# A decoder layer of 32 token groups: new engine orders and PSUM banks, head copies by DMA, GpSimd's small operations on ScalarE

## The chip, the cores and the metric

One core of a Trainium2 chip runs the whole kernel. The metric is the device time of one execution in microseconds (us).

## The reference, cut to what matters

x is 128 x 64 x 128 in float32 (128 sequences of 64 tokens, 128 channels), and so is the context.

```python
x = x + self_attention(layernorm(x))          # 16 heads of 8, RoPE, causal, softmax, output projection
x = x + cross(layernorm(x), ctx)              # Q K^T / dk, no softmax, times V; Wo; residual; layernorm with gain
x = x + ffn(layernorm(x))                     # 8 experts, top 1: h = relu(xhat_e W1_e^T + b1); y = x + h W2_e^T + b2
# in RoPE a head's 8 channels are two halves of 4: (x1 cos - x2 sin, x1 sin + x2 cos)
# in ffn: assign = argmax(x @ centroids.T), alpha = sigmoid(x @ centroids.T), out = alpha*y + (1 - alpha)*x
```

## The kernel before, in words

The 8192 tokens are 32 groups (`NG`) of 256 tokens (`J` = 2 tiles of 128 rows). The first two thirds of the program treat the groups; the rest is the feed-forward part, 71 blocks of 128 rows each, gathered by expert from a DRAM buffer `expert_rows` and scattered to the output.

Every engine has a function `one(g)`, a list of lines `stage(g, back, op)`, which `rounds` repeats: in round i an engine carries out each op for group i - back, in the order of the list. So a group passes through about nine rounds, and the order of the list is the order of the engine's program. Engines meet only by semaphores: `wait(engine, steps, group, "name")` waits until the named step of that group is done. The tables `BANK` (which of the 8 PSUM banks an op uses), `BEFORE` and `DRAIN` (whose reads must be over before a bank is written) belong to one order of the lists.

What happens to a group, with the names that the profile shows:

- SyncE's queue (SPq) loads x (`load_x`, tile `xin`), x again for the residual (`load_again`, `xr`) and the context (`load_ctx`, `cin`). Its function `late_loads(i)` runs after `one` in round i: three constants at i = 0, ten loads of biases and cross weights at i = 1 (semaphore `d_bias`), the mask `mk` and four others at i = 4, and one expert weight of 256 KB in each of the rounds 10 to 25.
- VectorE (DVE) takes the statistics (`stats_x`), ScalarE (ACT) and GpSimd (POOL) normalise, TensorE (PE) turns x (`x_turned`) and makes Q and K (`queries_keys`).
- DVE multiplies with cos and sin (`rotate`) and swaps partner partitions by a shuffle (`partners`, tile `t_`), POOL adds the two (`rotated`, tile `qk`).
- ACT makes four copies of `qk` (`by_head`, tile `ex`), each with the rows of three heads in four multiplied by 0 (`own4`), which spreads the heads for TensorE's tiles.
- PE builds the scores twice: once for the row maxima (`max_scores`, in front L691 and L701), which DVE reduces (`row_max`, L1432), and once with the maxima subtracted (`scores`, L733, L739, L747), which ACT exponentiates (`exp`, tile `prob`). `weighted` (L764) multiplies with V (tile `vau`, written by `values`, L678); DVE turns it back, POOL divides, `projected` (L791, L795) makes the output.
- Cross attention (`ctx_turned`, `cross_keys_values`, `values_keys`, `x1_turned`, `cross_queries`, `attended`, `cross_output`) and routing (`affinities`, `largest`, `ranks`, slot numbers, `scatter_rows`) follow in later rounds. Small tiles of 128 x 2 (variances, their roots) are worked on by POOL: `std_x`, `std_x1`, `std_y`, `std_x2`.

Two waits stand early in the program. PE's `constants()` runs inside `queries_keys` of group 1 and needs the ten loads of `d_bias`. DVE's `setup(4)` reads the mask.

Of the kernel before, what the change touches and what calls it, by code (L numbers as in the profile page):

```python
# [144 lines left out]
def decoder_kernel(nc, x, ctx, mask, wself, wcross, bcol, brow, cent, w1t, lngb, b1c, w2t, b2r,  # L145
# [17 lines left out]
    with es:  # L163
# [11 lines left out]
        WQ, WQR, WK, WKR, WV, WO = (ws[:, i, :] for i in range(6))  # L175
# [21 lines left out]
        own4, own4s = cf[:, o:o + 4], cf[:, o + 4:o + 8]  # L197
# [71 lines left out]
        sc = two("sc", [P, J, 3])  # L269
        tm = two("tm", [P, J, 3, E])  # L270
# [74 lines left out]
        ac_f = stage_steps("act_front", "xT | V0 V1 | x0 x1 x2 x3 | hi")  # L345
        ac_a = stage_steps("act_exp", "e0 | e1")
        ac_t = stage_steps("act_cross", "cT | kv | n | xT | Q2 | A | s0 s1")
        ac_r = stage_steps("act_route", "id | ea al1 | neg")
# [6 lines left out]
        dv_r = stage_steps("dve_route", "w0 w1 | b0 b1 a0 a1 | ab | af | g | i0 i1 | f | o | al | rk | tot | pr | sl | si")  # L355
        po_l = stage_steps("pool_norm_x", "eps pow")
        po_f = stage_steps("pool_front", "qk | lo")
        po_a = stage_steps("pool_attention", "n0 n1")
        po_t = stage_steps("pool_cross", "eps neg pow mr | x1b | eps2 std pow2 | zg")
        po_r = stage_steps("pool_route", "eps eps2 pow | R mr | z")  # L360
        d_x = [sem(f"dma_x{i}") for i in range(2)]
        d_xr = [sem(f"dma_x_again{i}") for i in range(2)]
        d_c = [sem(f"dma_ctx{i}") for i in range(2)]
        d_s = [sem(f"dma_scatter{i}") for i in range(2)]
# [18 lines left out]
        s_clear = sem("setup_cleared")  # L383
# [39 lines left out]
        def rounds(one, count, early=None):  # L423
# [11 lines left out]
            "x_turned": bank[6],  # L435
            "x1_turned": bank[4],
            "cross_keys_values": bank[7],
            "ranks": bank[6],
            "cross_queries": bank[4],
            "ctx_turned": bank[5],  # L440
            "queries_keys": bank[7],
            "attended": bank[6],
            "max_rows": bank[4],
            "projected": bank[5],
# [4 lines left out]
            "cross_output": bank[4],  # L449
            "values_keys0": bank[5],  # L450
            "values_keys1": bank[6],
            "weighted": bank[7],
            "values": bank[4],
# [9 lines left out]
        N_CONST, N_BIAS, N_LATE, N_WEIGHTS = 3, 10, 4, 2 * E  # L463
# [3 lines left out]
        SETUP = bank[3]  # L467


        EARLY_AT = (NG - 4, NG - 1, NG, NG + 1, NG + 2, NG + 3)  # L470
# [8 lines left out]
        def _(sp):  # L479
# [96 lines left out]
        def _(pe):  # L576
# [11 lines left out]
                "x_turned": [(dv_t, "mt", -3), (ac_t, "A", -5), (dv_r, "tot", -7), (ac_f, "xT", -1)],  # L588
                "x1_turned": [(ac_f, "V1", 3), (dv_t, "y1", -1), (ac_s, "x", 1), (ac_t, "Q2", -1),
                    (ac_t, "xT", -1)],  # L590
                "cross_keys_values": [(dv_a, "ot", -1), (dv_f, "k2", 1), (ac_t, "kv", -1)],
                "ranks": [(ac_f, "xT", 6), (dv_t, "mt", 3), (ac_t, "A", 1), (dv_r, "tot", -1)],
                "cross_queries": [(ac_t, "xT", 0), (ac_f, "V1", 3), (dv_t, "y1", -1), (ac_s, "x", 1),
                    (ac_t, "Q2", -1)],
                "ctx_turned": [(dv_t, "mt", -3), (dv_t, "x1", -4), (ac_t, "cT", -1)],
                "queries_keys": [(ac_t, "kv", -2), (dv_a, "ot", -3), (dv_f, "k2", -1)],
                "attended": [(dv_r, "tot", -2), (ac_f, "xT", 4), (dv_t, "mt", 1), (ac_t, "A", -1)],
                "max_rows": [(ac_t, "Q2", -2), (ac_t, "xT", -2), (ac_f, "V1", 1), (dv_t, "y1", -3),
                    (ac_s, "x", -1)],
                "projected": [(ac_t, "cT", 3), (dv_t, "mt", 0), (dv_t, "x1", -1)],  # L600
                "scores0": [(dv_s, "m0", 0), (ac_a, "e0", -1)],
                "scores1": [(dv_s, "m0", 0), (ac_a, "e0", -1)],
# [1567 lines left out]
```

## Time and profile before

| | |
|---|---|
| runs | 604.33, 600.85, 602.0 us; median 602.0 |
| profiled execution | 606.41 us, of which the span is 604.2 |
| TensorE, granted clock | 0.981 of full speed over the span |
| busy shares | PE 90%, DVE 80%, ACT 77%, POOL 72% |
| first and last group's first `weighted` on PE | at 31.98 and 423.94 us |

Times inside the span count from its start. Between the first and the last of these `weighted` lie 31 rounds; what follows is the feed-forward part. The engines' busy shares are means over both.

### The profile page before, as it was taken

To read this page: it belongs to the slowest core of one execution; us is meant where nothing else is said; L and a number is where in the kernel's file an instruction comes from. 1 tells how busy PE (TensorE), PEld (TensorE's weight loads), DVE (VectorE), ACT (ScalarE), POOL (GpSimd) and SP (SyncE) were. 2 spreads that over 40 slices of the span, in tenths; PEclk is the share of its full clock that TensorE was granted. 3 is DMA by queue.
4 is the path that set the end of the run, shared out by engine and by line. 5 is a ranking of instruction groups with operands and counts; after the bars stand their busy time and mean duration, and the time that the engine had idled before them with its cause. 6 is when DMAs were issued, how large, how long until landed. Compare 5 with 4: busy or idle time off the path is not lost.

```text
span 604.2 us, 26574 instructions
## 1 busy us (share of the span) xinstructions
PE 543.7 (90%) x8719; PEld 430.0 (71%) x8719; DVE 485.4 (80%) x1762; ACT 463.6 (77%) x1304; POOL 434.1 (72%) x852
## 2 busy tenths in 40 slices
PE   4789999999999999999999999978887988999995
PEld 2467767766766666676676666756786977999894
DVE  3787999888998989998899998987676666777673
ACT  2777777877888878888778787775776775899893
POOL 3334788888988989888998888877665566354553
PEclk9799999999999999999999999999899999999999
DMA  6421111322112312122111121102112122322210
GB/s 174 56 77 30 29 38 39 96 68 58 54 56 78 88 56 56 55 84 81 55 38 40 51 62 38 30 20 71 28 47 60 52 65 70 83 72 67 60 54 14
DMA packets 55189, 35.46 MB, mean 59 GB/s; under 512 B 14976, under 2 KB 50433, under 8 KB 55056
## 3 DMA queue, kind: packets, MB, share of 16 engines
q1 hardware_dynamic: 50160, 24.44, 15.5%
q0 software_dynamic: 4320, 8.66, 4.3%
q8 instruction: 74, 1.21, 0.8%
q10 hardware_dynamic: 576, 0.66, 0.4%
q14 instruction: 59, 0.48, 0.3%
HBM read 24.46 MB, written 9.74 MB: 57 GB/s over the span
## 4 chain that ended last, share of the span: by engine, by line
PE 84%; issue 6%; ACT 3%; DVE 3%; SPq 1%; another core or an unknown queue 1%; DVEq 1%; DMA 0%; POOLq 0%; POOL 0%; ACTq 0%
PE side L963 9%; PE side L764 8%; PE quad L701 6%; PE side L668 5%; PE quad L733 5%; PE side L948 5%; PE quad L948 5%; PE side L825 5%; PE side L678 3%; PE side L861 3%; PE side L879 3%; PE side L833 2%; PE side L795 2%; PE quad L747 2%; PE side L846 2%
## 5 line engine op out<-in xcount | busy, mean ns | idle before, releaser
L2046 POOL DMA_INDIRECT out<-yo,rb x71 | 69.9, 984 | 74.9 <-DVE yo L1784 45.6
L963 PE MATMUL side<-w,hT 128*128 x568 | 79.5, 284 | 8.7 <-DVE hT L1574 6.8
L1073 ACT ACTIVATE ex<-qk,cf 128x512 f32<-128x512 f32 x128 | 85.4, 718 | 0.0
L1432 DVE TENSOR_REDUCE mx<-quad 128x16 f32<-128x1024 f32 x64 | 75.3, 1218 | 10.9 <-PE quad L701 10.8
L963 PEld LDWEIGHTS side<-w,hT 128*128 128x128 f32 x568 | 71.5, 197 | 11.6 <-issue 11.0
L2013 POOL DMA_INDIRECT expert_rows<-pay,sli x64 | 68.6, 1072 | 12.8 <-issue 12.8
L1092 ACT ACTIVATE prob<-quad 128x1024 f32<-128x1024 f32 x64 | 62.1, 1022 | 18.6 <-PE quad L747 18.6
L764 PE MATMUL side<-prob,vau 128*32 128x64 f32 x2048 | 50.9, 223 | 14.5 <-issue 12.6
L764 PEld LDWEIGHTS side<-prob,vau 128*32 128x32 f32 x2048 | 36.7, 109 | 24.9 <-issue 17.0
L1564 DVE TENSOR_SCALAR xh<-rb 128x128 f32<-128x128 f32 x71 | 25.1, 354 | 27.8 <-issue 24.4
L1189 ACT COPY w1b<-w 128x512 f32 x71 | 43.7, 617 | 0.0
L948 PE MATMUL quad<-xhT,w1b 128*128 128x128 f32 x288 | 40.6, 287 | 2.0 <-issue 2.0
L1167 ACT ACTIVATE xhT<-quad,gb 128x128 f32<-128x128 f32 x71 | 33.2, 468 | 11.0 <-PE quad L931 7.4
L948 PEld LDWEIGHTS quad<-xhT,w1b 128*128 128x128 f32 x288 | 37.4, 202 | 2.3 <-issue 2.2
L1046 ACT COPY xT<-side 128x256 f32<-128x256 f32 x32 | 11.9, 372 | 35.2 <-PE side L659 35.2
L948 PE MATMUL side<-xhT,w1b 128*128 128x128 f32 x280 | 37.8, 278 | 1.0 <-ACT xhT L1167 1.0
L701 PE MATMUL quad<-ex,qk 32*64 32x256 f32 x1024 | 38.4, 396 | 0.1
L668 PE MATMUL side<-xT,ws 128*128 128x256 f32 x128 | 36.1, 405 | 1.8 <-ACT xT L1046 0.7
L948 PEld LDWEIGHTS side<-xhT,w1b 128*128 128x128 f32 x280 | 35.1, 196 | 1.7 <-ACT xhT L1167 1.2
L733 PE MATMUL quad<-ex,qk 32*64 32x256 f32 x1024 | 35.8, 387 | 0.2 <-DVE vau L1330 0.2
L1985 POOL TENSOR_TENSOR pay<-ve,half 128x4 f32<-128x4 f32 x32 | 33.4, 1042 | 2.7
L1197 ACT ACTIVATE bs<-rb 128x128 f32<-128x128 f32 x71 | 35.1, 495 | 0.0
(276 smaller groups left out, 1610.2 us busy)
## 6 DMA issues: line engine op xcount, KB each, us to landing
rb<-expert_rows SPq DMA_DIRECT2D x71, 68.0 KB
xin<-in_x SPq DMA_DIRECT2D x32, 128.0 KB
cin<-in_ctx SPq DMA_DIRECT2D x32, 128.0 KB
xr<-in_x SPq DMA_DIRECT2D x32, 128.0 KB, 2.3
w<-in_w1t SPq DMA_DIRECT2D x8, 256.0 KB
w<-in_w2t SPq DMA_DIRECT2D x8, 256.0 KB
out<-yo,rb POOLq DMA_INDIRECT x71
expert_rows<-pay,sli POOLq DMA_INDIRECT x64
```

The source lines that it names most:

```text
L668: last = mm(BANK["queries_keys"][:, i * TG:(i + 1) * TG], w, xT[g.par][:, :], start=True, stop=True)
L701: last = mm(quad[64 * b:64 * b + 64, r_, 256 * j:256 * j + 256], qk[g.par][strip, 0, own], ex[g.par][strip, :, 1, own], start=False, stop= ...
L733: mm(quad[64 * b:64 * b + 64, r_, 256 * j:256 * j + 256], qk[g.par][strip, 1, own], ex[g.par][strip, :, 0, own], start=j == 0, stop=False, ...
L764: last = mm(to[32 * i:32 * i + 32, j, :, r_, :], vau[g.par][:, j, 4 * r_ + i, :], prob[g.par][:, r_, (4 * j + i) * SQ:(4 * j + i + 1) * SQ ...
L948: last = mm(HT[u][c // 2][:, (c % 2) * P:(c % 2 + 1) * P], w1b[u][:, c * P:(c + 1) * P], xhT[u][:, :], start=True, stop=True)
L963: last = mm(YB[u][:, 0:D], hT[u][:, c, :], w2[:, bass.ds(e, 1), c, :], start=c == 0, stop=c == FC - 1)
L1073: act(ex[g.par][:, i, :, :].rearrange("p a t -> p (a t)"), qk[g.par][:, :, :].rearrange("p a t -> p (a t)"), ACT.Copy, scale=own4[:, i:i + ...
L1092: act(prob[g.par][:, 2 * h_:2 * h_ + 2, :], quad[:, 2 * h_:2 * h_ + 2, :], ACT.Exp).then_inc(*ac_a.done(f"e{h_}"))
L1189: cp(w1b[u][:, :], w1[:, bass.ds(e, 1), :].rearrange("p e f -> p (e f)")).then_inc(*ffn["act_w1"].done("act_w1"))
L1432: v.tensor_reduce(mx[g.par][:, 2 * h_:2 * h_ + 2, :], quad[:, 2 * h_:2 * h_ + 2, :].rearrange("p r (h k) -> p r h k", k=SQ), AX.X, ALU.max ...
L2013: v.indirect_dma_start(out=rows, out_offset=bass.IndirectOffsetOnAxis(ap=sli[g.par][:, j:j + 1], axis=0), in_=pay[g.par][:, j, :], in_offs ...
L2046: v.indirect_dma_start(out=o_rows, out_offset=bass.IndirectOffsetOnAxis(ap=number, axis=0), in_=yo[b.c % 4][:, :], in_offset=None, bounds_ ...
```

## The change: what it does

**Heads.** The columns of the Q and K weights are permuted on the chip when the means are subtracted, so that in a strip of 32 partitions head i holds the partitions i, i+4, i+8, ... The shuffle swaps partitions 16 apart instead of 4 apart, and the tables for cos, sin and the biases are loaded in that order, by eight DMAs on ACT's queue. ACT's four scaled copies per group are gone: `ex` is set to zero once, and four DMAs per group on SP's queue copy every fourth partition of `qk` into it (`by_head`).

**GpSimd's small operations.** Six operations of 128 x 2 per group (the additions of epsilon and one negation) go from POOL to ACT. The product of the affinity scores with their scales goes from one DVE operation to four small ones on ACT, `place` on DVE becomes a matmul in `ranks`.

**Orders.** All lists of stages are new, with the banks and their tables. ACT's stages stand one round later, DVE's one round earlier; the loads of SP move too.

```diff
+            def by_head(g):
+                first(sp, g, s_clear, 2)
+                wait(sp, pe_s, g.n - 2, "s3")
+                wait(sp, pe_a, g.n - 2, "s3")
+                wait(sp, po_f, g.n, "qk")
+                for i in range(4):
+                    sp.dma_start(ex[g.par][i:P:4, i, :, :], qk[g.par][i:P:4, :, :]).then_inc(d_by[g.par], 16)
             def one(g):
-                stage(g, 2, load_ctx)
-                stage(g, 3, load_again)
+                stage(g, 4, load_again)
                 stage(g, 0, load_x)
-            rounds(one, NG + 3, early=late_loads)
+                stage(g, 1, by_head)
+                stage(g, 0, load_ctx)
+            rounds(one, NG + 4, early=late_loads)
...
-                wait(pe, ac_f, g.n, "x3")
+                wait_dma(pe, d_by, g, 4)
...
+                wait(pe, dv_r, g.n - 1, "tot")
+                mm(bank_[:, 0:(J + 1) * E].rearrange("p (a e) -> p a e", e=E), identf,
+                   cnt[:, :].unsqueeze(1).broadcast_to((P, J + 1, E)), start=True, stop=False)
...
-            def by_head(g, part_):
...
-                for i in part_:
-                    act(ex[g.par][:, i, :, :].rearrange("p a t -> p (a t)"),
-                        qk[g.par][:, :, :].rearrange("p a t -> p (a t)"), ACT.Copy, scale=own4[:, i:i + 1]
-                        ).then_inc(*ac_f.done(f"x{i}"))
...
+            def var_x(g):
+                wait(ac, po_l, g.n - 2, "pow")
+                wait(ac, dv_l, g.n, "a1")
+                act(ve["L"][g.par][:, :], mv["L"][g.par][:, :, 1], ACT.Copy, bias=EPS).then_inc(*ac_v.done("eL"))
...
-            ac.dma_start(cf[:, 0:i0], consts[:, 0:i0]).then_inc(d_rope, 16)
-            ac.dma_start(bc[:, :], bcol).then_inc(d_rope, 16)
+            for r_ in range(4):
+                own = slice(32 * r_, 32 * r_ + 32)
+                ac.dma_start(cf[own, 0:4 * SQ], consts[own, 0:4 * SQ].rearrange("(i m) c -> m i c", i=4)
+                             ).then_inc(d_rope, 16)
+                ac.dma_start(bc[own, 0:4], bcol[own, 0:4].rearrange("(i m) c -> m i c", i=4)).then_inc(d_rope, 16)
+            ac.dma_start(cf[:, 4 * SQ:i0], consts[:, 4 * SQ:i0]).then_inc(d_rope, 16)
+            ac.dma_start(bc[:, 4:6], bcol[:, 4:6]).then_inc(d_rope, 16)
...
-                                 [p ^ (HD // 2) for p in range(32)]).then_inc(*dv_f.done("sh"))
+                                 [p ^ 16 for p in range(32)]).then_inc(*dv_f.done("sh"))
...
-            def scaled_scores(g):
...
-                v.tensor_tensor(tm[g.par][:, :, :, :],
...
-                u = ve["L"][g.par]
                 wait(po, ac_l, g.n - 2, "n")
-                wait(po, dv_l, g.n, "a1")
-                v.tensor_scalar(u[:, :], mv["L"][g.par][:, :, 1], EPS, None, ALU.add).then_inc(*po_l.done("eps"))
```

**TensorE's order.** The first rows are a piece of one steady round of before, in program order (L846 is `values_keys`, L764 `weighted`, L678 `values`, L691 and L701 `max_scores`, L659 `x_turned`).

```order
L846 MATMUL side<-kv_0 64x64 x7
L764 MATMUL side<-prob,vau 32x2x32 [waits act_cross_kv,dve_front_q1,dve_attention_ot,act_front_V0,act_exp_e0]
L764 MATMUL side<-prob,vau 32x2x32 x15
L678 MATMUL side<-ws,xT 128x128 [waits act_cross_Q2,act_cross_xT,act_maxima_x,act_front_V0,dve_cross_y1,act_front_xT]
L764 MATMUL side<-prob,vau 32x2x32 [waits act_exp_e1]
L764 MATMUL side<-prob,vau 32x2x32 x15
L691 MATMUL quad<-late_k,row_q 128x8x32 x7
L701 MATMUL quad<-ex,qk 64x256 [waits act_front_x0]
L659 MATMUL side<-cf,xn 128x128 [waits dve_route_tot,act_cross_A,act_front_xT,dve_cross_mt,act_norm_x_n]
```

The next rows are a piece of a steady round of the changed kernel; its lines are some five higher (L866 `attended`, L851 `values_keys`, L877 to L884 `cross_output`, L769 `weighted`, L696 and L706 `max_scores`, L782 `ctx_turned`, L664 `x_turned`, L683 `values`).

```order
L866 MATMUL side<-q_0,mt_0 64x64 x7
L851 MATMUL side<-kv_0 64x64 x7
L877 MATMUL side<-bo,ones_b 128x304 [waits dve_cross_x1]
L880 MATMUL side<-gc,xT_0 128x16 x2
L884 MATMUL side<-wcx,av 128x136 [waits act_cross_A]
L769 MATMUL side<-prob,vau 32x2x32 [waits act_cross_A,act_front_V0,act_exp_e0]
L769 MATMUL side<-prob,vau 32x2x32 [waits act_exp_e1]
L696 MATMUL quad<-late_k,row_q 128x8x32 [waits act_exp_e1,act_exp_e0]
L706 MATMUL quad<-ex,qk 64x256 [waits dma_by_head1]
L782 MATMUL side<-cf,cin 128x128 [waits dve_cross_y1,dma_ctx1]
L664 MATMUL side<-cf,xn 128x128 [waits dve_cross_mt,act_norm_x_n]
L683 MATMUL side<-ws,xT 128x128 [waits dve_attention_ot,act_front_xT]
```

`values` has left the gap between the two halves of `weighted`, `attended` and `values_keys` stand together, and the wait of `max_scores` for ACT's copy x0 is a wait for the DMAs of `by_head`.

**SP's queue at the start.** These are its first loads in the kernel before.

```order
L516 DMA xin<-in_x 128x2x128
L487 DMA cf<-in_consts 128x279
L487 DMA nkf<-in_negk 128x64
L493 DMA br<-in_brow 128x768
L493 DMA wcx<-in_wcross 128x512
L493 DMA gc<-in_cent 128x8
L493 DMA ln_c<-in_brow 128x1 x3
L495 DMA wop<-in_wself 32x1x128 x4
```

And these, after the first two loads of x and the constants, are those of the changed kernel.

```order
L541 DMA ex<-qk 32x512 [waits pool_front_qk,setup_cleared_heads]
L541 DMA ex<-qk 32x512 x3
L530 DMA cin<-in_ctx 128x2x128
L493 DMA br<-in_brow 128x768
L493 DMA wcx<-in_wcross 128x512
L493 DMA gc<-in_cent 128x8
L493 DMA ln_c<-in_brow 128x1 x3
L495 DMA wop<-in_wself 32x1x128 x4
```

The ten loads of `d_bias` stand behind the copies of group 0, which wait for `rotated` of group 0.

**The mask.** This piece is SP's queue of the changed kernel in its round 4, up to the mask (the copies are those of group 3).

```order
L516 DMA xin<-in_x 128x2x128 [waits act_norm_x_n]
L541 DMA ex<-qk 32x512 [waits pool_front_qk,pe_attention_s0,pe_scores_for_max_s0]
L541 DMA ex<-qk 32x512 x3
L530 DMA cin<-in_ctx 128x2x128 [waits pe_cross_cT]
L500 DMA mk<-in_mask 128x64x16
L502 DMA gb<-in_lngb 128x16
```

And this is DVE's program of the changed kernel around its first use of the mask (the shuffle is that of group 3).

```order
L1514 TENSOR_TENSOR x_0<-side,xr 128x256 [waits pe_cross_out,dma_x_again0]
L1528 TENSOR_TENSOR mt_1<-side,headmask 128x256 [waits pe_cross_gram]
L1471 STREAM_SHUFFLE t__1<-t__1 128x512 [waits dve_front_q1,pool_front_qk]
L1741 TENSOR_REDUCE pen<-mk 128x64 [waits dma_mask]
L1743 TENSOR_SCALAR pen<-pen 128x64 [waits setup_mask]
L1387 CAST part<-br 128x256
L1491 STREAM_TRANSPOSE ot<-side 128x512 [waits pe_attention_p1]
```

In before the mask's load had only loads of x and context ahead of it. Now copies that wait for POOL, and a load that waits for PE's `ctx_turned` of group 2, stand ahead of it.

## Rows read from the trace of the kernel before

**Rows 1.** The page: the chain that ended last, share of the span by engine

```profile
PE 84%; issue 6%; ACT 3%; DVE 3%; SPq 1%; another core or an unknown queue 1%; DVEq 1%; DMA 0%; POOLq 0%; POOL 0%; ACTq 0%
```

**Rows 2.** PE's timeline (start, us, what): the first group's weighted, the last one's

```profile
31.98 0.65 PE L764 MATMUL side<-prob,vau 128*32 128x64 f32 x32 [0.75 <-ACT prob L1092]
...
423.94 1.11 PE L764 MATMUL side<-prob,vau 128*32 128x64 f32 x42
```

**Rows 3.** The chain in one round, 252.4 to 265.1: start, us, what

```profile
253.29 1.10 PE side L668 x4
...
259.37 0.59 PE side L764 x28
259.95 0.45 issue
260.40 0.33 PE side L764 x4
260.73 0.64 PE side L678 x4
...
263.34 0.37 PE side L659 x2
263.71 0.22 PE side L808 x2
```

**Rows 4.** Windows: the same round; busy PE, PEld, DVE, ACT, POOL; PEclk, DMA share

```profile
252.50:265.00 12.50, 11.89 (x237) 8.69 (x235) 11.24 (x42) 10.16 (x29) 11.24 (x25) 1.00 0.23 67
```

**Rows 5.** Waits of DVE and PE, 120 to 360, 19 rounds: us, times, longest

```profile
DVE ot L1442 <- PE side L764: 7.0, 17, 0.5
DVE mx L1432 <- PE quad L701: 6.3, 19, 0.9
DVE y L1492 <- PE side L879: 4.9, 19, 0.4
...
PE side L764 <- issue: 8.3, 19, 0.5
```

**Rows 6.** Groups by line: busy us, mean ns of one, idle before

```profile
L1073 ACT ACTIVATE ex<-qk,cf 128x512 f32<-128x512 f32 x128 | 85.4, 718 | 0.0
L1159 ACT ACTIVATE ea<-ea 128x2 f32<-128x2 f32 x32 | 6.5, 204 | 1.0
L1903 POOL TENSOR_SCALAR ve_L<-mv_L 128x2 f32<-128x2 f32 x32 | 7.6, 237 | 5.2 <-DVE mv_L L1298 5.2
L1517 DVE TENSOR_TENSOR tm<-y,sc 128x48 f32<-128x48 f32 x32 | 6.9, 216 | 0.0
```

**Rows 7.** SP's queue and DVE's use of xin in a round that loads weights

```profile
256.93 0.47 SPq L516 DMA_DIRECT2D xin<-in_x  x1
257.44 0.47 SPq L509 DMA_DIRECT2D w<-in_w1t  x1
...
261.11 0.49 DVE L1295 BATCH_NORM_STATS2 stat_L<-xin 128x6 f32<-128x128 f32 x2 [0.35 <-DMA xin<-in_x]
```

**Rows 8.** DMA issues: KB each, median us from issue to landing

```profile
xr<-in_x SPq DMA_DIRECT2D x32, 128.0 KB, 2.3
...
mk<-in_mask SPq DMA_DIRECT2D x1, 512.0 KB, 6.9
```

**Rows 9.** The start: SP's bias loads, first and last, and POOL's first qk

```profile
3.17 0.47 SPq L493 DMA_DIRECT2D br<-in_brow  x1
...
6.06 2.87 SPq L495 DMA_DIRECT2D wop<-in_wself  x4
...
16.26 1.27 POOL L1915 TENSOR_TENSOR qk<-t__0 128x512 f32<-128x512 f32 x1 [5.43 <-DVE t__0 L1422]
```

**Rows 10.** The start on PE (constants) and DVE (shuffle, mask)

```profile
19.68 0.77 PE L649 MATMUL quad<-ws,bvx 128*128 128x128 f32 x2 [2.75 <-ACT tri_b L1033]
...
30.85 0.73 DVE L1422 STREAM_SHUFFLE t__0<-t__0 128x512 f32<-128x512 f32 x1
...
32.38 1.21 DVE L1718 TENSOR_REDUCE pen<-mk 128x64 f32<-128x1024 int32 x1
```

More of the change, by code:

```diff
@@ L174, in decoder_kernel @@
         ws = sb("ws", [P, 6, D])
-        WQ, WQR, WK, WKR, WV, WO = (ws[:, i, :] for i in range(6))
+        WQP, WKP, WV, WO = (ws[:, i, :] for i in (1, 3, 4, 5))
         wcx = sb("wcx", [P, 4 * D + E])
@@ L363, in decoder_kernel @@
         d_c = [sem(f"dma_ctx{i}") for i in range(2)]
+        d_by = [sem(f"dma_by_head{i}") for i in range(2)]
         d_s = [sem(f"dma_scatter{i}") for i in range(2)]
@@ L434, in decoder_kernel @@
             "max_scores3": bank[3],
-            "x_turned": bank[6],
-            "x1_turned": bank[4],
-            "cross_keys_values": bank[7],
-            "ranks": bank[6],
[L439 to L444, printed above, removed]
+            "ctx_turned": bank[4],
+            "x_turned": bank[5],
+            "values": bank[7],
+            "x1_turned": bank[6],
+            "cross_keys_values": bank[4],
+            "ranks": bank[6],
+            "queries_keys": bank[5],
+            "cross_queries": bank[7],
+            "max_rows": bank[6],
             "scores0": bank[0],
@@ L448, in decoder_kernel @@
             "scores3": bank[3],
-            "cross_output": bank[4],
+            "projected": bank[4],
+            "attended": bank[7],
             "values_keys0": bank[5],
             "values_keys1": bank[6],
+            "cross_output": bank[4],
             "weighted": bank[7],
-            "values": bank[4],
         }
@@ L896, in one @@
                 stage(g, 4, max_scores)
+                stage(g, 4, ctx_turned)
                 stage(g, 2, x_turned)
+                stage(g, 3, values)
                 stage(g, 6, x1_turned)
@@ L1727, in _ @@
             v.memset(row_q[:, :, :, :], 0.0)
-            v.memset(row_kk[:, :, :, :], 0.0).then_inc(s_clear, 1)
-            rounds(one, NG + 4, early=setup)
+            v.memset(row_kk[:, :, :, :], 0.0)
+            v.memset(ex[0][:, :, :, :], 0.0).then_inc(s_clear, 1)
+            rounds(one, NG + 3, early=setup)
             def last_table(k):
@@ L1870, in _ @@
             rows_in(Block(2))
-            place(g28)
+            own_rank(g28)
             counted(g28)
@@ L1909, in rotated @@
             def rotated(g):
-                wait(po, ac_f, g.n - 2, "x3")
+                wait_dma(po, d_by, g.back(2), 4)
                 wait(po, pe_s, g.n - 2, "s3")
```

353 lines of the change are left out of this document (169 added, 184 removed).

## The prediction

> **What bounds the kernel now.** I read the chain first: TensorE (PE) holds 84% of it and "issue" 6% [rows 1], so the time is PE's program, and no other engine's wait runs through it for long. Next I took the timeline, to see how the span divides. The first group's `weighted` stands at 31.98 and the last one's at 423.94 [rows 2]: 31 rounds of 12.64 us, a start of 32 and a feed-forward tail of 180 us. The change leaves the tail's matmuls alone, so three numbers matter: the start, the length of a round, and whether the tail keeps its 180.
>
> For the round I took the chain over one of them. Its pieces add up to 12.55, nearly all PE, with one "issue" of 0.45 in the middle of `weighted`, behind which four matmuls take 0.33 [rows 3]. It comes back in every round [rows 5]. Nothing that the profile knows of is missing there, so I read it as instructions that come late. In the same 12.5 us DVE is busy for 11.24, ACT for 10.16, POOL for 11.24 [rows 4]. The waits say how near DVE is: over 19 rounds it stands still for 7.0 + 6.3 + 4.9 = 18.2, about 1.0 per round [rows 5], so its own work, gaps between instructions included, takes 11.5. A change that shortens PE's round has 1.0 us before it meets DVE.
>
> **The rounds, part by part.** *ACT.* Four copies of 718 ns go [rows 6], 2.9 us per round. Ten operations of 128 x 2 or x 8 come, at 204 ns like its own small ones [rows 6], 2.0. ACT goes from 10.2 to 9.3 and does not bind, either way. *POOL* loses six operations at about 237 ns [rows 6], 1.4 us, and goes from 11.24 to below 10. *DVE* loses two of at most 216 ns [rows 6]: 11.5 - 0.4 = 11.1. That is the floor that DVE sets.
>
> *PE.* The order has 12 changes of tile shape per round before and 9 after, counted along both lists. What one costs I read from two turnings of a tile that are alike: L659 behind a shape change 0.37, L808 behind its own kind 0.22 [rows 3], so 0.15. I priced every group anew by whether it now stands behind its own shape. `x_turned` saves 0.15; `values`, 0.64 between two halves of `weighted` and now behind `x_turned`, 0.19; the second half of `weighted`, `values_keys`, the turned maxima and `cross_queries` 0.11 to 0.16 each (0.56). `ctx_turned`, the output's bias and that of `cross_output` now follow a change and pay 0.15 + 0.11 + 0.06. Of the 1.10 of `queries_keys` (L668), 0.22 was a wait for the bank of the cross keys, which it leaves. The matmul added to `ranks` costs 0.18. The sum is -0.15 - 0.19 - 0.56 + 0.32 - 0.22 + 0.18 = -0.62, and the round becomes 11.93. This keeps the "issue" and its slow matmuls, 0.45 + 0.33 less the 0.1 that four matmuls cost elsewhere. If they vanish, PE needs 11.3 and DVE's 11.1 is next.
>
> The Trainium skill, in the page "TensorEngine Tiling (Array Packing)", section Key Properties, says that a change of the tiling mode, not merely of the tile, drains TensorE. The 0.15 in [rows 3] agrees. By the rule alone one would price only the three changes fewer, 0.45, and with the added matmul the round would become 12.28; this is the last rival below.
>
> *The queue.* The four copies are now DMAs on SP's queue, and there they stand ahead of the next load of x. This closes a loop of exactly one round: `rotated` of a group ends, four issues at 0.51 from start to start [rows 7] make 2.0, `load_ctx` 0.5, `load_again` 0.5, then x takes 2.3 from issue to landing, as the residual's load of the same size does [rows 8]. DVE's statistics wait for it, and in DVE's new list everything up to `partners` stands behind them: 4.2 by its operations. Then POOL's 1.3 for `rotated` [rows 9], and the loop is closed: 2.0 + 0.5 + 0.5 + 2.3 + 4.2 + 1.3 = 10.8. That is below 11.93 and costs nothing. In the 16 rounds that load an expert's weights one more issue of 0.5 stands in it, and landing is slower: in such a round x went out at 256.93 and DVE stood until 261.11, 4.2 us [rows 7]. The loop is then 11.3 with a landing of 2.3 and 13.2 with one of 4.2. I take 12.2, between the two, since the weights now go out 1.0 ahead of x instead of behind it. The mean round is (15 x 11.93 + 16 x 12.2) / 31 = 12.07, bounds 11.3 and 12.6. The rounds give back 31 x (12.64 - 12.07) = 17.7 us.
>
> **The start, part by part.** *Biases.* The ten loads went out from 3.17 to 8.9 [rows 9], long before PE's constants at 19.68, which waited for something else [rows 10]. Now they stand behind the copies of group 0, which wait for POOL's `qk`. That ended at 17.5 [rows 9]; ACT issues eight more DMAs ahead of its first work at 0.5 to 0.7 each (the last four bias loads, with the same kind of pattern, took 2.87 [rows 9]), so I put it at 21.5. Then 2.0 for the copies, 0.5 for the context, 5.8 for the ten loads and 2.3 for landing: 32.1. PE's constants stand in `queries_keys` of group 1, ahead of the first `max_scores`. All behind them is late by 32.1 - 19.7 = 12.4, so the first `weighted` comes at 44. Bounds: 8 if ACT's DMAs delay nothing, 17 if the biases land as slowly as the mask's 6.9 [rows 8].
>
> *The mask.* DVE read it at 32.38 without a wait [rows 10]. Now DVE wants it right behind the shuffle of group 3, and its load stands behind the copies of the same group, which wait for what POOL makes of that very shuffle: 1.3 + 2.0 + 0.5 + the landing of 6.9 [rows 8] = 10.7 of standstill on DVE, more if `ctx_turned` of group 2, for which the context's load waits, is late. Behind it in DVE's program are the turned outputs and the next row maxima, for which PE and ACT wait soon; about 1.7 are hidden by PE's rest of a round. I take 9, bounds 6 and 14.
>
> *Back.* The first eight rounds have fewer operations than a steady one, and a program that is late by its latencies catches up in them a little: -3, an estimate, bounds 0 and -6. The start costs 12.4 + 9 - 3 = 18.4, bounds 10 and 28.
>
> *The tail* holds the same matmuls; the leftover small operations change places only. Zero, within 2 us either way, covered by PE's own chain there.
>
> **The sum.** 606.4 (the profiled execution) + 18.4 - 17.7 = 607.1. The profiled execution lies 4.4 above the median of the runs, so against the median it is 602.0 + 0.7: about 602, no change that can be measured. A measurement of this kernel tells a change from none at about 0.5%, 3 us.
>
> **The rivals.**
> - *The rounds save more, or the start costs less (faster).* If the missing instructions were a matter of the old order, PE drops to 11.3; coupled to DVE's 11.1 the round is about 11.5, and 31 x 1.14 = 35 are saved: 602 - 35 + 18 = 585. If only the start is cheaper, at its bound of 10, 594. For it speaks that the stall comes once in each of 19 rounds, always in `weighted` [rows 5], and the new order has other neighbours there; against it, that the two halves of `weighted` and the 48 matmuls behind them now follow each other without a pause. Chance 0.24.
> - *SP's queue sets the round (slower).* The place is `load_x` behind the four copies, the price is what the loop has beyond PE's 11.93. From a mean round of 12.64 - 18.4/31 = 12.05 on the kernel is slower. With the landing of 4.2 in weight rounds (13.2) and 11.93 else, the mean is 12.6 and the time 602 - 1 + 18 = 619; half of that excess gives 610. For it: DVE already stood for x once in such a round [rows 7]. Against it: x's load was last in the queue before weights then. Chance 0.22.
> - *The shape's grouping gives only its three drains.* Round 12.28, so 31 x 0.36 = 11 saved, 602 - 11 + 18 = 609; 615 if the stall of 0.45 grows in the now longer dense stretch by 0.2. For it: the groups' first matmuls overlap with the drain of the group ahead, so savings of 0.1 to 0.2 may be read twice. Chance 0.14.
>
> **How the numbers follow.** The forecast (start 15 to 22, round 11.9 to 12.2) has 0.40 and runs from 594 to 609, with 602 its middle: 0.13 of it below 599, 0.15 within 3 us of the 602, 0.12 above. The first rival lies from 580 to 594 nearly whole. The second covers 606 to 620, the third 605 to 616. Faster: 0.24 + 0.13 = 0.37. Same: 0.15 + 0.04 from the low ends of the others and 0.03 from the high end of the first = 0.22. Slower: the rest, 0.41. The range takes in all of the forecast and leaves out a tenth at either end: 586 to 617.
>
> **What the profile of the changed kernel would show.** The first `weighted` near 44 instead of 31.98, and PE's constants near 32 waiting for the bias loads; DVE's reduction of the mask behind a wait of about 10 us for its DMA, and PE idle by it. Rounds of 11.9 to 12.2 from the first `weighted` to the last; DVE's waits for PE down to 0.8 per round; in weight rounds a wait of the statistics for x. In the chain L659 at 0.22, L678 at 0.45 and "issue" of 0.45 near `weighted`. I am wrong if the first `weighted` stands below 38 or above 50, if the rounds lie below 11.7 or above 12.3, or if DVE has the mask when it asks for it.

## The result

The changed kernel takes 671.0 us (median of 667.07 to 673.08) against 603.16 for the kernel before on the same chip: a ratio of 1.112, 95% interval 1.106 to 1.119. The forecast of 602 was wrong, and so was its range. Its profiled execution has a span of 670.6 us, 66.4 longer than before.

The page of the changed kernel shows first that no single engine holds the end any more: PE's share of the chain is 39% where it was 84% [rows 1], and SP's queue, DMA, DVE and POOL have a part in it.

```profile
PE 548.1 (82%) x8783; PEld 444.6 (66%) x8783; DVE 490.5 (73%) x1701; ACT 439.2 (65%) x1496; POOL 388.6 (58%) x659
...
PE 39%; DVE 17%; issue 14%; SPq 10%; DMA 8%; POOL 5%; ACT 3%; ACTq 2%; DVEq 2%; another core or an unknown queue 0%; POOLq 0%
```

Next the timelines of its start (start, duration, engine, line): SP's copies and bias loads, PE's constants, the first `weighted`, DVE's reduction of the mask, and POOL's first `qk`.

```profile
22.60 2.44 SPq L541 DMA_DIRECT2D ex<-qk  x4
...
28.60 2.90 SPq L495 DMA_DIRECT2D wop<-in_wself  x4
...
32.94 0.79 PE L654 MATMUL side<-ws,bvx 128*128 128x128 f32 x2 [9.95 <-DMA wop<-in_wself]
...
44.78 0.65 PE L769 MATMUL side<-prob,vau 128*32 128x64 f32 x32 [0.62 <-ACT prob L1088]
...
68.18 1.22 DVE L1741 TENSOR_REDUCE pen<-mk 128x64 f32<-128x1024 int32 x1 [11.32 <-DMA mk<-in_mask]
...
21.25 1.27 POOL L1927 TENSOR_TENSOR qk<-t__0 128x512 f32<-128x512 f32 x1
```

All of this came as the prediction had it, within a microsecond: constants at 32.9 (forecast 32.1), first `weighted` at 44.8 (44), DVE's wait for the mask 11.3 (10.7). In part that is luck: POOL's `qk` ended at 22.5 instead of 21.5 and the copies took 2.4 instead of 2.0, but PE could start 1.4 us behind the last issue, where 2.3 stood. The larger error lies behind it. I took the start of each group's first `weighted` from PE's timeline and split the span by them, here with the kernels of the experiments:

| kernel | first `weighted` | next five rounds, us | mean of the 26 rounds behind | median, us | ratio to before, interval |
|---|---|---|---|---|---|
| before | 32.0 | 63.1 | 12.65 | 603.2 | |
| changed | 44.8 | 83.2 | 13.98 | 671.0 | 1.106 to 1.119 |
| e1_early | 40.7 | 76.0 | 13.56 | 657.7 | 1.085 to 1.094 |
| e2_queue | 35.8 | 75.5 | 13.78 | 646.9 | 1.062 to 1.076 |
| e3_one_copy | 44.8 | 80.7 | 13.20 | 654.4 | 1.076 to 1.094 |
| e5_scores_late | 35.6 | 81.1 | 13.58 | 656.7 | 1.084 to 1.094 |
| e6_queue_plus32 | 36.2 | 78.2 | 13.82 | 657.6 | 1.086 to 1.099 |
| e7_before_plus32 | 33.3 | 65.6 | 13.43 | 625.4 | 1.029 to 1.042 |
| e8_queue_half | 35.8 | 76.5 | 13.72 | 645.1 | 1.062 to 1.076 |
| e9_before_half | 33.0 | 62.3 | 12.56 | 600.7 | 0.995 to 1.000 |
| e10_split | 36.1 | 76.6 | 12.97 | 632.1 | 1.041 to 1.050 |
| e11_split_first | 36.4 | 77.4 | 12.70 | 626.7 | 1.032 to 1.042 |
| e12_start | 30.5 | 76.0 | 12.72 | 618.9 | 1.023 to 1.029 |
| e13_before_dense | 33.3 | 73.5 | 14.67 | 669.4 | 1.106 to 1.118 |
| e14_spread | 31.9 | 78.2 | 14.03 | 662.3 | 1.089 to 1.101 |
| e15_quarter_shift | 35.9 | 74.7 | 12.66 | 621.6 | 1.022 to 1.027 |

The three columns ahead of the median are of one execution, the profiled one; the executions of one kernel lie up to 10 us apart, and the profiled one is the longest for changed, e2_queue and e8_queue_half and the shortest for e1_early. The time in e3_one_copy, e8_queue_half, e9_before_half and e15_quarter_shift is that of a kernel that leaves work out.

From before to changed that is +12.8 (start), +20.1 (five rounds, the stop for the mask among them), +34.7 (26 rounds), and -1.1 in the tail, together the 66.4 us between the spans. The steady rounds hold half of it, and I had forecast them 0.6 shorter instead of 1.3 longer.

The chain of the changed kernel in one of these rounds (start, us, what) goes through matmuls for only 2.2 us of it:

```profile
253.88 1.24 POOL qk L1927
255.19 0.47 SPq L541
...
257.61 0.58 SPq L530
258.24 0.47 SPq L511
258.75 0.43 SPq L523
259.23 4.87 DMA xin<-in_x
264.19 0.49 DVE stat_L L1341 x2
...
265.37 0.43 PE side L877
265.80 0.67 PE side L880 x4
266.47 1.11 PE side L884 x4
...
268.10 0.76 DVE t__1 L1471 x2
...
269.21 1.23 POOL qk L1927
```

This is the loop that the prediction described as a rival: `qk`, four copies, context, weights, residual, x, statistics, shuffle, `qk` again, 15.3 us here. Its copies take 2.4 (2.0 forecast), x takes 4.9 from its issue (3.2 taken). Between statistics and shuffle stands a piece that the prediction did not have, PE's `cross_output` (L877 to L884), for which DVE waits ahead of `y`. The granted clock was 0.52 from 263.5 to 267.5; at full speed the same matmuls took 1.2 instead of 2.2. Not every round goes this way: in the chain from 120 to 149, around a round of 13.0, SP's queue has no part; it runs over PE's list and the row maxima. The waits of the changed kernel from 150 to 400, 18 rounds, say how DVE meets it, and show a second item:

```profile
DVE stat_L L1341 <- DMA xin<-in_x: 36.8, 18, 3.1
...
PE quad L752 <- issue: 20.5, 49, 0.5
PE side L877 <- DVE x L1514: 9.3, 10, 1.3
```

PE loses 20.5 us in 18 rounds, 1.1 per round, in the last matmuls of `scores` (L752), in pieces of less than 0.5, for nothing that the profile knows ("issue"; I call these late instructions). Before, it was one such piece per round [rows 5].

### The profile page after: what moved, and what is told of

The parts are those of the page before. It is cut to its first block, busy times and chain, and to the rows that moved or that the text cites. A ratio compares the mean times of both kernels' runs of the same rounds, so it can differ in the third digit from the quotient of the medians.

```text
span 670.6 us, 26792 instructions
## 1 busy us (share of the span) xinstructions
PE 548.1 (82%) x8783; PEld 444.6 (66%) x8783; DVE 490.5 (73%) x1701; ACT 439.2 (65%) x1496; POOL 388.6 (58%) x659
## 4 chain that ended last, share of the span: by engine, by line
PE 39%; DVE 17%; issue 14%; SPq 10%; DMA 8%; POOL 5%; ACT 3%; ACTq 2%; DVEq 2%; another core or an unknown queue 0%; POOLq 0%
DMA xin<-in_x 8%; PE side L970 7%; SPq L541 5%; PE side L955 4%; PE quad L955 4%; PE quad L738 3%; DVE mx L1481 3%; POOL qk L1927 3%; SPq L530 2%; PE quad L752 2%; PE quad L706 2%; PE side L769 2%; DVE x L1514 1%; PE quad L939 1%; PE side L800 1%
## 5 line engine op out<-in xcount | busy, mean ns | idle before, releaser
L1088 ACT ACTIVATE prob<-quad 128x1024 f32<-128x1024 f32 x64 | 65.6, 1026 | 65.9 <-PE quad L752 65.9
L2015 POOL DMA_INDIRECT expert_rows<-pay,sli x64 | 64.3, 1004 | 34.4 <-DVE sli L1652 22.2
L1481 DVE TENSOR_REDUCE mx<-quad 128x16 f32<-128x1024 f32 x64 | 73.9, 1195 | 4.1 <-PE quad L706 3.9
L1916 POOL TENSOR_TENSOR rs_L<-ve_L,half 128x2 f32<-128x2 f32 x32 | 22.3, 698 | 62.6 <-ACT ve_L L1148 62.6
L752 PE MATMUL quad<-shift,pick 32*128 32x128 bf16 x512 | 30.3, 221 | 30.8 <-issue 30.0
L1341 DVE BATCH_NORM_STATS2 stat_L<-xin 128x6 f32<-128x128 f32 x64 | 15.5, 284 | 51.2 <-DMA xin<-in_x 50.9
L1935 POOL TENSOR_TENSOR mt<-mx,mt 128x32 bf16<-128x32 f32 x64 | 14.8, 252 | 53.7 <-ACT mt L1081 53.7
L752 PEld LDWEIGHTS quad<-shift,pick 32*128 32x128 bf16 x512 | 15.8, 92 | 43.9 <-issue 43.6
L769 PE MATMUL side<-prob,vau 128*32 128x64 f32 x2048 | 38.1, 229 | 1.1 <-ACT prob L1088 1.0
L738 PE MATMUL quad<-ex,qk 32*64 32x256 f32 x1024 | 35.9, 386 | 3.6 <-issue 2.9
L706 PE MATMUL quad<-ex,qk 32*64 32x256 f32 x1024 | 38.4, 405 | 0.0
L683 PE MATMUL side<-ws,xT 128*128 128x128 f32 x128 | 21.2, 290 | 20.1 <-issue 16.0
```

The costliest lines, as they stand in the source:

```text
L706: last = mm(quad[64 * b:64 * b + 64, r_, 256 * j:256 * j + 256], qk[g.par][strip, 0, own], ex[g.par][strip, :, 1, own], start=False, stop= ...
L738: mm(quad[64 * b:64 * b + 64, r_, 256 * j:256 * j + 256], qk[g.par][strip, 1, own], ex[g.par][strip, :, 0, own], start=j == 0, stop=False, ...
L752: last = mm(quad[:, r_, :].rearrange("p (j i q) -> p j i q", j=J, i=4)[:, :, i, :], pick[strip, i, :, :].rearrange("p b k -> p (b k)"), sh ...
L769: last = mm(to[32 * i:32 * i + 32, j, :, r_, :], vau[g.par][:, j, 4 * r_ + i, :], prob[g.par][:, r_, (4 * j + i) * SQ:(4 * j + i + 1) * SQ ...
L1088: act(prob[g.par][:, 2 * h_:2 * h_ + 2, :], quad[:, 2 * h_:2 * h_ + 2, :], ACT.Exp).then_inc(*ac_a.done(f"e{h_}"))
L1481: v.tensor_reduce(mx[g.par][:, 2 * h_:2 * h_ + 2, :], quad[:, 2 * h_:2 * h_ + 2, :].rearrange("p r (h k) -> p r h k", k=SQ), AX.X, ALU.max ...
```

## The experiments

**e1_early: the early loads alone.** The edit sends the ten bias loads in round 0 and the mask in round 2.

```diff
-                if i == 1:
+                if i == 0:
                     for dst, src in ((br[:, :, :]
...
+                if i == 2:
+                    sp.dma_start(mk[:, :, :], m_rows).then_inc(d_mask, 16)
```

> The changed kernel with the ten bias loads sent in round 0 and the mask in round 2; the copies keep their place in SP's queue. Both theories: DVE's 9.2 and 11.3 us of waiting at the start (for the second load of x behind the bias loads, and for the mask) go, the first weighted comes near 34 instead of 44.8, and the time falls by 20 to 27 us to 644 to 651. The rounds behind it stay at 14.1 us. If the time falls by less than 10, the early loads were not what made the start late.

It gave 13 us where 20 to 27 were expected (657.7, not 644 to 651). In the changed kernel 28.1 us lie between the second and the third group's `weighted`; here it is 16.0. But the first `weighted` only came to 40.7, and each of the first five rounds still takes 15.2 us on average. So in the new order the first rounds are slow by themselves (12.6 before). The steady rounds, 13.56 here against 13.98, differ by about as much as executions of one kernel do.

**e2_queue: the loop through SP's queue cut.** The copies stand one round later in the queue, so that the next x goes out ahead of them (which also frees the biases); the mask goes in round 2.

```diff
-                stage(g, 1, by_head)
+                stage(g, 2, by_head)
```

> The changed kernel with the copies by DMA one round later in SP's queue, so that the load of x for the next group goes out ahead of them, and the mask in round 2. Theory 1 (the one-round loop through SP's queue sets the round at 14.1; PE alone, with its late instructions, needs 12.8): first weighted near 34, rounds of 12.8, time 605 to 613. Theory 2 (the loop is the chain from the row maxima over ACT and POOL back to PE's scores inside one round, the queue only fills the gap): rounds stay at 13.7 to 14.1, time 640 to 650, as the first kernel of this call. DVE's wait for x should vanish under both.

The wait of DVE for x vanished, yet the time is that of theory 2, and theory 2 is wrong as well: PE now hardly waits for anyone. Its waits from 150 to 400, 19 rounds:

```profile
PE quad L753 <- issue: 23.0, 51, 0.7
PE side L721 <- POOL mt L1936: 1.2, 4, 0.5
```

The rounds are of two kinds. In 14 of the 26 steady ones PE's granted clock is at full speed or within 0.03 of it, and they take 13.2 on average; in the other 12 it is 0.83 to 0.91 on average, and they take 14.5. Windows show it (length, busy time of PE, PEld, DVE, ACT, POOL, then PE's clock as a share of full speed, DMA share, GB/s): one quick round, one slow round, and four pieces of the slow one.

```profile
261.86:274.54 12.68, 11.42 (x237) 8.86 (x237) 10.69 (x40) 9.33 (x37) 9.73 (x18) 1.00 0.28 86
274.54:288.85 14.31, 12.94 (x237) 10.22 (x236) 11.03 (x41) 10.01 (x40) 9.96 (x19) 0.88 0.25 77
282.00:283.50 1.50, 0.78 (x20) 0.34 (x13) 1.50 (x6) 0.46 (x1) 1.20 (x2) 1.00 0.35 119
283.50:285.00 1.50, 0.85 (x14) 0.59 (x14) 0.37 (x3) 0.15 (x1) 1.48 (x3) 0.92 0.16 49
285.00:286.50 1.50, 1.50 (x17) 1.27 (x17) 0.43 (x2) 0.96 (x2) 0.94 (x2) 0.50 0.00 0
...
288.00:289.50 1.50, 1.50 (x52) 1.37 (x56) 0.62 (x5) 1.11 (x5) 0.81 (x2) 0.94 0.00 0
```

From 282 to 285 PE is busy for 1.63 us of 3, with late instructions in between; then the granted clock is 0.50, the lower level (1.2 instead of 2.4 GHz), until some 288, and the round is 1.6 longer. The Trainium skill, "TensorE: Matmul & The Clock Gate", Part 1, says that the clock follows how busy the array has been; these rows agree. Late instructions don't always bring the clock down: the quick round has the same three pieces, from 269.9 to 271.6, and the clock stays at 1.00. In PE's timeline of that round the late instructions look so:

```profile
282.96 0.21 PE L753 MATMUL quad<-shift,pick 32*128 32x128 bf16 x1 [0.39 <-issue]
283.68 0.25 PE L753 MATMUL quad<-shift,pick 32*128 32x128 bf16 x3 [0.51 <-issue]
284.40 0.34 PE L753 MATMUL quad<-shift,pick 32*128 32x128 bf16 x9 [0.47 <-issue]
```

So under the queue's loop lay a second floor of nearly the same height: PE alone, 12.68 in a quick round with 1.3 of stalls in it, 13.8 in the mean with the slow rounds.

**e3_one_copy: the queue's loop made shorter.**

```diff
-                for i in range(4):
+                for i in range(4 if g.n < 2 else 1):
```

> The changed kernel, but from group 2 on only one of the four copies per group is made (work left out: three quarters of the spread heads keep the values of groups 0 and 1). The queue's loop loses three issues, 1.9 us, and some of the transfer ahead of x. Theory 1: the start stays (44.8), DVE's wait for x shrinks, rounds of about 12.8, time near 635. Theory 2 (chain over the maxima): no change, 668 to 673.

DVE's wait for x fell from 36.8 to 4.8 us, and the rounds from 13.98 to 13.20, many of them 12.6: the loop does hold the changed kernel, and PE's own floor is next. Theory 1 holds in kind; its size was too good (654.4, not 635), and the clock explains little of that, as only 4 of the 26 rounds have it low.

**e5_scores_late: PE's list changed behind the maxima.**

```diff
-                stage(g, 4, scores)
                 stage(g, 5, projected)
                 stage(g, 6, attended)
+                stage(g, 4, scores)
```

> The second kernel of this call with projected and attended moved ahead of scores in PE's list, so that 20 more matmuls stand between the maxima and the scores, and the many short matmuls of scores stand right ahead of values_keys. If the late instructions (three times 0.47 us in the last matmuls of scores) belong to that run of short matmuls, they stay there, and the time is that of the second kernel within 4 us. If they come from the place in the round, they move to other lines and shrink, and the time is 8 to 15 us below it.

Neither: it is 10 us above e2_queue. `projected` now has to wait for ACT's copy of the cross keys and values, and `cross_output` for one of ACT's, 2.0 us per round; the late instructions are gone, and the clock is at full speed in all but one of the 26 rounds. PE's timeline there:

```profile
257.94 0.28 PE L797 MATMUL side<-bo,ones_b 128*128 128x256 bf16 x1 [1.45 <-issue]
...
259.21 1.43 PE L739 MATMUL quad<-ex,qk 32*64 32x256 f32 x32
...
260.80 0.39 PE L753 MATMUL quad<-shift,pick 32*128 32x128 bf16 x16
```

The same 16 matmuls take 0.39 in one piece once PE has waited ahead of them. (The 1.45 stands as "issue", but ends 0.05 behind the end of ACT's copy `kv` at 257.89, for which the bank of `projected` waits.) The round is 13.30 with 2.0 of waits in it: PE's own work is 11.3, the number that the prediction gave for a round without late instructions.

**e6 to e9: is it the number of instructions?** In the quick rounds of e2_queue 487 PE instructions take 12.69 us, in before 483 take 12.50; both 26 ns each. That suggested a supply at a fixed mean rate. Two kernels get 32 small matmuls more per group, two lose half of `weighted`.

```diff
                 free(g, "max_rows")
+                for _ in range(32):
+                    mm(BANK["max_rows"][:, 0:8], ident_b[:, :], ident_b[:, 0:8], start=True, stop=True)
```

```diff
-                    for j in range(J):
+                    for j in range(J if g.n < 2 else 1):
                         for i in range(4):
                             last = mm(to[32 * i:32 * i + 32, j, :, r_, :], vau[g.par][:, j, 4 * r_ + i, :],
```

> The kernel e2_queue with 32 more matmuls of 8 columns per group in max_rows (they write columns that are written again; 64 more PE instructions beside 487 per round). Theory S (PE's instructions come at a mean rate of 26 ns each, 12.69 us for 487 as in the undisturbed rounds of e2_queue and 12.50 for 483 in before, whatever they cost in the array): rounds longer by 64 x 0.026 = 1.66 us, so +51 us over 31 rounds, near 698. Theory W (the work in the array counts, a bf16 matmul of that kind takes some 0.02 us with its weights): +0.6 us per round, +20 us, near 667.

> The kernel before with the same 32 small matmuls per group. Theory S: rounds 12.65 + 1.66 = 14.3, time near 654, and the late instructions (0.45 us per round in weighted) stay or grow. Theory W: the 0.45 us of idle time take up a part, rounds of 12.7 to 13.2, time 606 to 622.

> The kernel e2_queue with the second half of weighted left out from group 2 on (work left out: half of the products with V; 64 PE instructions fewer, 0.5 us of the array's time). Theory S: rounds 12.69 - 1.66 = 11.0, held up by DVE at 11.2 to 11.5, the stalls of 3 x 0.47 gone and with them the granted clock of 0.5 behind them; time 570 to 580. Theory W: rounds 13.78 - 0.5 = 13.3, time near 632.

> The kernel before with the same half of weighted left out. Theory S: the late instructions vanish, PE falls below DVE's own 11.5, rounds 11.5 to 11.8, time 568 to 578. Theory W: rounds 12.65 - 0.5 = 12.15, time near 588.

The mean rate is refuted; e6 and e8 miss the other expectation too (657.6 against 667, 645.1 against 632). With 64 instructions more, before's time is 625.4, just above what the count of work gave, and its round grows by 0.78, about what they cost in the array (32 in 0.94 there), not by 1.66, and its one late piece stays 0.45. With 64 fewer, e2_queue keeps its three pieces at the same place, the clock is low in 17 of 26 rounds instead of 12, and the rounds at full speed are no shorter (13.2). In e6 they move: L741, the first matmuls of `scores`, takes 3.06 for 32 instead of 1.05, nothing is late behind it, and the clock is low in 1 round of 26. e9 shows something else. With 0.5 us of work less on PE the kernel before stays at 12.56 a round, and its waits from 150 to 400 are elsewhere:

```profile
DVE pay L1504 <- POOL sc L1968: 7.6, 19, 0.4
DVE ont L1455 <- POOL on L1933: 7.5, 15, 1.0
```

The chain there, in a steady round, has no matmul in it:

```profile
228.07 0.34 DVE pay L1504
...
229.83 0.49 DVE stat_T L1295 x2
...
231.25 0.69 POOL rs_T L1947
...
239.37 0.72 POOL sc L1968
240.58 0.34 DVE pay L1504
```

DVE waits for the last of POOL's list, POOL for DVE's statistics, and this loop of two engines is 12.51 long. In before, then, DVE and POOL stand right behind PE, and half a microsecond less on PE gives nothing that matters (ratio 0.995 to 1.000).

**e10_split, e11_split_first: other neighbours for the late matmuls.** `scores` is cut in two, with its last 16 matmuls (`shifted`) behind `projected`; in e11 behind `attended` too, and ACT copies `attended` ahead of its first exponential.

This is the list of e11_split_first.

```diff
                 stage(g, 4, scores)
                 stage(g, 5, projected)
                 stage(g, 6, attended)
+                stage(g, 4, shifted)
                 stage(g, 4, values_keys)
                 stage(g, 6, cross_output)
```

> The kernel e2_queue with scores cut in two: its last 16 matmuls (the ones with the three late instructions) stand behind projected, and attended behind values_keys. Theory D (the late instructions come where some 96 instructions are issued within 1.6 us, wherever they lie): the slower matmuls of projected break the run, the three stalls of 0.47 and the granted clock of 0.5 behind them go, rounds of 11.6 to 12.1, time 580 to 596. Theory P (they belong to these matmuls, or to this moment of the round): rounds stay at 13.4 to 13.9, time 638 to 650. If the stalls go but a wait for a copy of ACT takes their place, rounds of 12.5 to 13.

> As e10_split, but attended stands ahead of the last 16 matmuls too, and ACT copies its result ahead of the first exponential. Theory D: as e10_split, with the wait of cross_output for ACT gone and one of weighted's second half for its exponential (0.4 us) in its place; rounds of 11.5 to 12.0, time 578 to 594. Theory P: 638 to 650.

Neither theory. (The rounds of e10_split, 12.97, lie in its third range, but no wait for ACT makes them.) The late instructions do not go: in e11_split_first they fall into `projected` (L804), whose matmuls are longer and hide some of them, and into `attended`. The chain of one round there:

```profile
259.54 1.05 PE quad L739 x32
...
261.32 0.43 PE side L804 x3
261.75 0.34 issue
262.08 0.97 PE side L804
```

But the idle time is no longer in one place, and the clock stays at full speed (1.00 from 150 to 400, where e2_queue has 0.93); the time falls by 20 us by the medians. The steady round is 12.50 to 12.52, the same as before. The 26 rounds take 26 x (13.78 - 12.70) = 28 us less than in e2_queue, whose profiled execution is its longest. An estimate of the clock's part comes from e2_queue alone: twelve rounds with a low clock, 1.3 longer than the others, 16 us. The other 12 (13.2 against 12.7 in rounds at full speed) are the order's, and were not taken apart.

**e12_start: the start of the new order.** The eight rope loads go out on SP's queue instead of ACT's, and DVE's bias work stands behind its row maxima.

```diff
-                bias_parts(g.c)
...
                 stage(g, 3, row_max, 1)
+                bias_parts(g.c)
```

> The kernel e11_split_first with two repairs of the start: the eight DMAs of the rope tables go out on SP's queue instead of ACT's, and DVE's bias work of the first rounds stands behind its row maxima instead of ahead of all else. In e11_split_first the first weighted came at 35.6 us (32.0 in before) and the five rounds behind it took 77 us (63 in before). If the eight issues on ACT and the place of the bias work are what costs there, the first weighted comes at 31 to 33, the five rounds take 66 to 72, and the time is 612 to 619. If not, it stays at 624 to 628.

The first `weighted` came at 30.5, 5.9 earlier than the 36.4 of e11_split_first (the expectation has 35.6), about eight issues of 0.7 on ACT's queue. The five rounds behind it hardly changed (76.0 after 77.4). That doesn't clear the bias work: at its new place PE waits 3.5 us for its product `bkv` (L1405), and 4.9 in three waits for exponentials. What makes these rounds slow is not found. At 618.9 it is the quickest kernel in the new order that leaves nothing out, and still 2.3 to 2.9% slower than before.

**e13_before_dense: one swap in the kernel before.**

```diff
-                stage(g, 5, projected)
                 stage(g, 4, scores)
+                stage(g, 5, projected)
```

> The kernel before with one swap in PE's list: projected behind scores instead of ahead of it, so that scores follows max_rows directly, as in the changed kernel. If that closeness makes the late instructions, two or three stalls of 0.47 us appear in the last matmuls of scores (L747), PE's round grows by 0.5 to 1.0 us and the time to 615 to 635. If it does not, the time stays within 4 us of before (599 to 607).

669.4: this one swap costs as much as the whole change. Late instructions in L747 come to only 3.1 us in 17 rounds; instead `scores`, 1.6 us, now stands ahead of `projected`, and a loop closes through three engines. Its chain (start, us, what) in one round:

```profile
250.76 0.69 PE side L795 x4
...
251.57 0.43 DVE x L1465
252.03 0.49 DVE stat_T L1295 x2
...
253.45 0.69 POOL rs_T L1947
...
254.58 1.08 POOL expert_rows L2013
...
260.43 0.74 POOL on L1933 x2
...
261.98 0.68 PE side L861 x16
...
263.07 1.08 PE quad L733 x32
...
264.92 0.69 PE side L795 x4
```

`projected` gives DVE the new x, DVE the statistics, POOL their root; behind that root stands the rest of POOL's list, and in it `divide` (`on`); then DVE's steps up to `cnt`, for which `attended` (L861) waits, and behind that in PE's list `scores` and the next `projected`: 14.16 us round. No engine is busy for all of that round. The mean of 14.67 has nine rounds with a low clock in it, 15.2 against 14.4 for the others.

**e14_spread, e15_quarter_shift.** In the first, `queries_keys` (four slow matmuls) stands between the two halves of the first part of `scores`; in the second, 12 of the 16 last matmuls of e2_queue are left out.

```diff
                 stage(g, 4, scores)
+                stage(g, 2, queries_keys)
+                stage(g, 4, scores_of, 1)
                 stage(g, 5, projected)
```

```diff
-                for i in range(4):
+                for i in (range(4) if g.n < 2 else (3,)):
```

> The kernel e12_start with the first 32 and the last 32 fp32 matmuls of scores set apart by queries_keys (four slow matmuls, 0.97 us), so that no run of a hundred PE instructions is left there without a slow matmul. If such a run makes the late instructions, they vanish there, PE's round falls to 11.5 to 12.0, and the time from 619 to 592 to 605. If not, they turn up a little earlier or later, the round stays at 12.5 to 12.7 and the time at 615 to 622.

> The kernel e2_queue with 12 of the 16 last matmuls of scores left out from group 2 on (work left out: the row maxima are subtracted for one head in four only; 24 PE instructions and 0.25 us fewer per round). If the late instructions belong to these matmuls, at most one of 0.47 us is left, the granted clock stays at full speed and the time falls from 647 to 600 to 612. If they come wherever PE has run that long without a wait, they move on to projected or attended, and the time is 625 to 645.

e14 missed both times (662.3) and decides nothing on late instructions: `queries_keys` is 2 us later, DVE waits for it, POOL's low halves come late and PE waits for them; the loop over the maxima is 13.7 to 14.5. e15 does: three late pieces remain though 12 of the 16 matmuls are gone, now one in L753 and two in `projected`, as PE's timeline shows.

```profile
254.75 0.21 PE L753 MATMUL quad<-shift,pick 32*128 32x128 bf16 x1 [0.48 <-issue]
255.50 0.47 PE L801 MATMUL side<-wop,ont 128*128 128x128 f32 x2 [0.31 <-issue]
256.22 0.47 PE L801 MATMUL side<-wop,ont 128*128 128x128 f32 x2 [0.25 <-issue]
```

They do not belong to the matmuls of the shift. The time, 621.6, lies between what the two answers expected, and the clock stays up in 24 of 26 rounds.

## Why the prediction was wrong

- *The start* (biases, mask): right in place and size, +12.8 where 12.4 stood, a wait of 11.3 where 10.7 stood; e1_early, which takes both away, confirms the place and not the whole worth (13 us of the 20 to 27 expected then).
- *Back, -3*: wrong. The step "a program that is late by its latencies catches up" had no row. The first five rounds took 83.2 instead of 63.1; without the stop for the mask still 75 to 81 in each complete kernel of the new order. The whole start costs 32.9, not 18.4.
- *PE's round, 11.93*: the array's part was right (e5_scores_late: 11.3 without late instructions, as forecast). The step that failed is "this keeps the issue and its slow matmuls" at 0.45 + 0.33. The new order has three late pieces, 1.3 to 1.4 us, for one. They give back what the grouping saved: 12.68 for a full round of PE in e2_queue against 12.50. And behind them the clock falls, in 12 of the 26 rounds of e2_queue, 1.3 us each, and in 7 of 26 of the changed kernel, 0.9 each; the prediction had no term for that. A smaller slip stands ahead of it: 11.93 comes from a round of 12.55 and was compared with the mean of 12.64, which counts 31 x 0.09 = 2.8 us as saved for nothing.
- *The queue, 12.2 in weight rounds and nothing else*: the mechanism was right, as the second rival, and its size was not. Its copies cost 2.4, not 2.0, x lands in 4.9 and not in 3.2, and from there to the end of `qk` it takes 6.3, where I had 4.2 + 1.3 and nothing for PE's `cross_output` inside it. In the round shown the loop is 15.3. e3_one_copy shows it is a hold: 13.98 falls to 13.20 with three copies fewer. Without a weight load x landed in 2.7 (from 401.5), near the 2.3 assumed.
- *The floor that DVE sets, 11.1*: wrong in kind. e9_before_half shows that before is held at 12.5 by a loop over DVE and POOL as soon as PE is quicker; e13_before_dense shows how little slack there is. I took busy time plus idle time of one engine as its floor. The floor is the longest loop over several in-order lists, and the waits table of one engine doesn't show it while another engine is the slowest.
- *The third rival* (the grouping gives only its three drains) fell: the saving in the array is real, it is only not paid out. The page "TensorEngine Tiling (Array Packing)" of the Trainium skill, section Key Properties, was no worse for it than my own sum: by its rule with the 0.15 of the rows PE's round would have been 12.28, by my rows alone 11.93, and the measured 12.68 is above both because of the late pieces.

Of the 66 us, 12.8 are the late first `weighted`, some 7 the stop for the mask with what is given back behind it (83.2 - 76.0), some 13 the slow first rounds (76.0 - 63.1), and 34.7 the steady rounds, less 1.1 in the tail. Within those 34.7 two floors lie so close together (queue 13.6 in e1_early, PE with its clock 13.8 in e2_queue) that they can't be added up.

What stays open: what makes the late instructions. Shown is that they come in pieces of about 0.5 us, the first some 90 PE instructions behind the last slow matmuls in before and in e2_queue (there L839), and some 120 behind them in e6; that they move to other matmuls when the order changes or matmuls are left out (e11, e15); that neither 64 instructions more nor fewer elsewhere remove them (e7, e8); and that few are seen where PE has waited shortly ahead (e5, e13). That they are a matter of the instruction supply is argued only. Two rivals were not tested by an edit, and the traces speak against both. One is SP's transfers in the same stretch: e3_one_copy, with three copies fewer per group, still has 49 pieces from 150 to 400, 21.1 us in all. The other is the profile's transfers of kind `instruction` on queue 8, 16 KB each: in e2_queue the late pieces end anywhere from 0.4 to 8.1 us behind the start of the last one. Open too is why the first five rounds of the new order are slow.

## What to carry to other kernels

In a program of in-order engines that hand work around, each moved step closes or opens a loop over several lists: write down, for each engine's step, what releases it and what it releases a round later, and add the loop up with measured gaps before counting on busy times. One swap of two neighbouring steps cost 11% here. A copy that moves from an engine to a DMA queue takes its wait along: everything behind it in that queue then waits for the same event. And when a bound engine is made quicker by half a microsecond, try first, by leaving that work out, whether the round gets shorter at all.

## What the hardware showed unexpectedly

- TensorE's granted clock fell from full speed to 0.50 for some 3 us behind a stretch of 3 us in which PE was busy for 1.6, in the middle of rounds in which it is busy for 90% of the time. Such rounds took 14.5 on average and the others 13.2, so 16 us over the 26 rounds of e2_queue. The same late pieces one round earlier left the clock at full speed.
- TensorE's late instructions, three times in a row 0.4 to 0.5 us with one to four matmuls between them, did not go away with fewer instructions: 1.2 us per round with 487 (e2_queue) and with 423 (e8_queue_half).
- A DMA of 128 KB behind four of 64 KB within SBUF, two of 128 and one of 256 KB took 4.9 us from issue to landing, against 2.7 in a round without the 256 KB, and 2.3 for one of its size in before [rows 8].
